# Fourteen expert pieces of a spiking MetaFormer block set into the slots of its last gating groups

## What is computed

```
x = x + conv(ln_c(x))          # q, k, v = lif(xf @ W.T); attention without softmax; lif(y); lif(y @ Wp.T + bp)
t = tokens of x
xt = ln_t(t)
gate = softmax(xt @ Wg);  topv, topi = top_k(gate, 2);  topv = topv / (sum(topv) + 1e-6)
for e in range(8):
    h = gelu(xt @ W1[e] + b1[e])          # 128 -> 512
    ye = h @ W2[e] + b2[e]                # 512 -> 128
    out = out + ye * scores[:, e]
return t + out
```

## Time and profile before

| | |
|---|---|
| median of 3 runs | 544.33 us (542.35 to 544.41) |
| the profiled execution: its time and its span | 544.11 us, 542.4 us |
| TensorE busy, share | 345.3 us, 64% |
| VectorE | 400.4 us, 74% |
| ScalarE | 274.1 us, 51% |
| GpSimd | 221.6 us, 41% |
| mean granted TensorE clock | 0.776 of 2.4 GHz |

### The profile page before, as it was taken

The page is one execution under the profiler, slowest core; times in us unless marked ns, Lnnn a source line. Parts: engine busy times, 40 slices in busy tenths (PEclk is TensorE's granted clock), DMA queues, the critical chain, the costliest instruction groups (busy, mean ns, idle before and its releaser), DMA issues.

```text
span 542.4 us, 10627 instructions
## 1 busy us (share of the span) xinstructions
PE 345.3 (64%) x2516; PEld 285.8 (53%) x2516; DVE 400.4 (74%) x1384; ACT 274.1 (51%) x581; POOL 221.6 (41%) x233
## 2 busy tenths in 40 slices
PE   2456654654644766254420499999999999999200
PEld 2233232432422534133320399999999999999200
DVE  4799999999999599998862356666666666666186
ACT  3436362554525435243230267666677777666073
POOL 3000000007274017374777145566666666666400
PEclk9877677776776576655555599999999999999855
DMA  6901000002121012121354222222222222221299
GB/s 180 274 15 17 16 15 16 16 15 61 41 59 42 9 21 68 42 65 45 98 181 124 74 55 77 71 69 71 71 77 64 76 71 67 70 69 50 68 351 303
DMA packets 62123, 43.05 MB, mean 79 GB/s; under 512 B 29057, under 2 KB 56745, under 8 KB 62096
## 3 DMA queue, kind: packets, MB, share of 16 engines
q1 hardware_dynamic: 53648, 28.85, 20.2%
q0 software_dynamic: 6720, 12.97, 7.6%
q10 hardware_dynamic: 1728, 0.94, 0.6%
HBM read 22.09 MB, written 19.91 MB: 77 GB/s over the span
## 4 chain that ended last, share of the span: by engine, by line
PE 43%; DVE 42%; issue 4%; ACT 3%; POOL 3%; DMA 3%; ACTq 1%; POOLq 0%; SPq 0%; DVEq 0%
PE PS L1172 18%; DVE U L892 7%; DVE VV L884 7%; DVE H_all L872 6%; PE PS L1162 6%; PE PS L1164 5%; PE PS L1163 5%; DVE stats L630 3%; DVE KV L708 3%; POOL by_expert L427 3%; PE PS L1149 2%; PE PS L1105 2%; DVE X L1006 2%; DVE spikes L902 2%; DVE X L1010 1%
## 5 line engine op out<-in xcount | busy, mean ns | idle before, releaser
L427 POOL DMA_INDIRECT by_expert<-XG,place x98 | 97.3, 993 | 197.7 <-DVE place L794 169.3
L443 POOL DMA_INDIRECT by_token<-osp,target x112 | 119.5, 1067 | 89.9 <-DVE osp L976 55.9
L1172 PE MATMUL PS<-w_now,hid 128*128 128x128 f32 x896 | 108.8, 275 | 0.0
L1172 PEld LDWEIGHTS PS<-w_now,hid 128*128 128x128 f32 x896 | 104.8, 192 | 0.0
L560 ACT ACTIVATE hid<-PS,b1c 128x256 f32<-128x256 f32 x224 | 88.2, 480 | 5.1 <-PE PS L1164 2.9
L1162 PE MATMUL PS<-rows_high,w_high 128*128 128x256 f32 x224 | 69.1, 308 | 0.9 <-DVE rows_low L960 0.3
L1164 PE MATMUL PS<-rows_high,w_low 128*128 128x256 f32 x224 | 64.1, 286 | 0.0
L1163 PE MATMUL PS<-rows_low,w_high 128*128 128x256 f32 x224 | 64.0, 286 | 0.0
L566 ACT ACTIVATE w_now<-W_s 128x512 f32 x56 | 35.6, 635 | 54.5 <-PE PS L1172 45.5
L1042 PE MATMUL PS<-xT,wT 128*128 128x392 f32 x96 | 54.4, 693 | 0.7 <-ACT xT L488 0.7
L954 DVE CAST w_high<-H_all 128x512 fp32r x56 | 24.1, 431 | 40.0 <-PE PS L1164 38.7
(11 more groups left out here) (156 smaller groups left out, 570.7 us busy)
## 6 DMA issues: line engine op xcount, KB each, us to landing
rows_in<-by_expert SPq DMA_DIRECT2D x56, 130.0 KB, 2.1
...
```

The source lines that it names most:

```text
L427: pool.indirect_dma_start(by_expert, bass.IndirectOffsetOnAxis(ap=place[g % SENDING][:, k, r:r + 1], axis=0), XG[g % SENDING][:, r, :], No ...
L443: pool.indirect_dma_start(by_token, bass.IndirectOffsetOnAxis(ap=target[b][:, a:a + 1], axis=0), rows_out[b][:, a, :], None, bounds_check= ...
L1172: m = pe.matmul(PS[:, 4 + b % 2, a * 128:a * 128 + 128], hid[b % 2][:, hb, a * 128:a * 128 + 128], w2_now[b % 2][:, hb * C:hb * C + C], st ...
```

## The change

The first 14 pieces hold only rows of groups 0 to 2 (`EARLY` = 14, full pieces of 256 rows), and their loads wait for those groups' scatters alone. The plan is split: `plan_early` in the points of slot 13, `plan_late` in those of slot 21. In slot 16 the pieces 0 and 1 are set up and the `up` of piece 0 is made. Then `EARLY_SLOT` says which pieces stand in which slot: two in each of the slots 17 to 20, four in slot 21. The call for piece j holds the turning of the rows of piece j + 2, `up` of j + 1 and `down` of j. `SEND_SLOT` puts the sends of pieces 0 to 3 behind the scatter of group 7; the others follow the scatter of group 8. The pieces from 12 on follow behind the slots, written out one by one, without loops. In all pieces ScalarE now rounds rows and W1 (`round_rows`, `round_w1`), VectorE makes the remaining parts, and `down` takes W2 from where it lies, at an address from a register that TensorE loads itself; `set_w2` is gone. W1 is loaded in slot 15 into a part of `xT`, and 12 output tiles stand in the place of 4.

```diff
+    EARLY_SLOT = {BLOCKS + 1: (None, 0, None, 1), BLOCKS + 2: (None, 2, None, 3), BLOCKS + 3: (None, 4, None, 5),
+                  BLOCKS + 4: (None, 6, None, 7), BLOCKS + 5: (8, 9, 10, 11)}
+    SEND_SLOT = {BLOCKS + 4: range(0, 4)}
+    PLAN_SLOT, PLAN_FROM = norm2_slot[EARLY_GROUP] + 2, 6
+    SENT_EARLY = max(r.stop for r in SEND_SLOT.values())
+    assert END == BLOCKS + 6 and PLAN_SLOT < BLOCKS
+    def early(slot, k):
+        its = EARLY_SLOT.get(slot, ())
+        return [j for j in its[k:k + 1] if j is not None]
     assert all(norm2_slot[g] < norm2_slot[g + 1] for g in range(GATES - 1))
...
+        target = [sb(f"target{i}", [128, HALVES], I32) for i in range(PIECES)]
...
+            def load_piece(j):
+                start = sp.value_load(piece_start[0:1, j:j + 1], min_val=0, max_val=E * CAP)
+                if j >= DEEP:
+                    sp.wait_ge(piece_read, j - DEEP + 1)
+                sp.dma_start(rows_in[j % DEEP][:], by_expert[bass.ds(start, ROWS), :]
+                             .rearrange("(p a) c -> p a c", a=HALVES)).then_inc(piece_in[j % DEEP], 16)
...
             sp.wait_ge(pieces_ready, 1)
+            for g in range(EARLY_GROUP + 1):
+                sp.wait_ge(scattered[g % SENDING], sent_until(g + SENDING))
+            for j in range(EARLY):
...
+            sp.dma_start(by_expert[E * CAP:E * CAP + ROWS, :].rearrange("(p a) c -> p a c", a=HALVES),
+                         pad_rows[:]).then_inc(padded, 16)
+            sp.wait_ge(pieces_ready, 2)
             sp.wait_ge(padded, 16 * (E + 1))
             for i in range(SENDING):
                 last = max(g for g in range(GATES) if g % SENDING == i)
                 sp.wait_ge(scattered[i], sent_until(last + SENDING))
...
+            def send(j):
+                pool.wait_ge(piece_read, j + 1)
+                pool.wait_ge(rows_ready, j + 1)
+                for a in range(HALVES):
+                    pool.indirect_dma_start(by_token, bass.IndirectOffsetOnAxis(
+                        ap=target[j][:, a:a + 1], axis=0), rows_out[j % OUTS][:, a, :], None,
+                        bounds_check=last_row, oob_is_err=False).then_inc(rows_sent[j % OUTS], 16)
...
             for slot in range(-1, END):
                 for g in gate_group(slot, 2):
                     scatter(g)
-
-
-            last_row = pool.alloc_register("last_row")
-            pool.reg_mov(last_row, 2 * TOK - 1)
...
+            def round_w1(j):
+                act.wait_ge(pieces_ready, 1 if j < EARLY else 2)
+                if j >= 2:
+                    act.wait_ge(up_done, HB * (j - 1))
+                e = expert_on_act(j)
+                nc.scalar.activation(w1_high[j % 2][:], W1_s.rearrange("p e h -> p (e h)")[:, bass.ds(e * HID, HID)],
+                                     ACT.Copy).then_inc(w1_rounded, 1)
+            def gelu(j):
+                e = expert_on_act(j)
+                if j >= 2:
+                    act.wait_ge(down_done, j - 1)
+                for hb in range(HB):
+                    act.wait_ge(up_done, HB * j + hb + 1)
+                    nc.scalar.activation(hid[j % 2][:, hb, :], up_bank(j, hb), ACT.Gelu,
+                                         bias=b1c[:, bass.ds(e * HB + hb, 1)]).then_inc(gelu_done, 1)
...
+            def round_rows(j):
+                act.wait_ge(piece_turned, j + 1)
+                if j >= 2:
+                    act.wait_ge(up_done, HB * (j - 1))
+                nc.scalar.activation(rows_high[j % 2][:], turn_bank(j), ACT.Copy).then_inc(rows_rounded, 1)
+            def piece_on_act(j):
+                if j + AHEAD < PIECES:
+                    round_rows(j + AHEAD)
+                if j + 1 < PIECES:
+                    gelu(j + 1)
+                if j + 3 < PIECES:
+                    round_w1(j + 3)
             for slot in range(-1, END):
                 if slot < 0:
                     spread(0, 0)
...
+                if slot == BLOCKS:
+                    act.wait_ge(w1_in, 16)
+                    for j in range(AHEAD):
+                        round_w1(j)
+                    round_rows(0)
+                    piece_on_act(-1)
+                for j in early(slot, 1):
+                    piece_on_act(j)
+                if slot > BLOCKS:
+                    for x_ in norms(slot):
+                        spread(*x_)
+                for j in early(slot, 2):
+                    piece_on_act(j)
                 if slot >= 0:
                     for x_ in norms(slot):
                         normalise(*x_)
                 for it in ring[slot][1]:
                     copy_item(it)
...
+            def piece_stage(j, stage):
+                n, b = j + AHEAD, (j + AHEAD) % 2
+                if stage == 4:
+                    if j >= 1:
+                        add_b2(j - 1)
+                elif n >= PIECES:
+                    return
+                elif stage == 0:
+                    v.wait_ge(rows_rounded, n + 1)
+                    v.tensor_tensor(rows_low[b][:], turn_bank(n), rows_high[b][:].bitcast(F32),
+                                    ALU.subtract).then_inc(piece_copied, 1)
+                elif stage == 1:
+                    e = expert_on_vector(n)
+                    v.wait_ge(w1_rounded, n + 1)
+                    v.tensor_tensor(w1_low[b][:], W1_s.rearrange("p e h -> p (e h)")[:, bass.ds(e * HID, HID)],
+                                    w1_high[b][:].bitcast(F32), ALU.subtract).then_inc(w1_set, 1)
+                elif stage == 2:
+                    v.scalar_tensor_tensor(target[n][:], rows_in[n % DEEP][:, :, C + 1], piece_rank[:, n:n + 1],
+                                           rows_in[n % DEEP][:, :, C], ALU.not_equal, ALU.add).then_inc(piece_read, 1)
...
+            def point_work(slot, point):
+                norm_stage(slot, point)
+                gate_stage(slot, point)
+                if slot == PLAN_SLOT:
+                    plan_early(point - PLAN_FROM)
+                if slot == BLOCKS and point == 15:
+                    v.wait_ge(pieces_ready, 1)
+                    v.wait_ge(w1_in, 16)
+                if slot == BLOCKS and point >= 16:
+                    piece_stage((point - 16) // 4 - AHEAD, point % 4)
+                for j in early(slot, point // 6):
+                    piece_stage(j, point % 6)
+                if slot == END - 1:
+                    plan_late(point - PLAN_FROM)
...
+            def down(j, a):
+                e = pe.value_load(piece_expert[0:1, j:j + 1], min_val=0, max_val=E - 1)
+                w2 = W2_s[:].rearrange("p e b c -> p (e b c)")
+                if a == 0:
+                    if j >= 2:
+                        pe.wait_ge(rows_ready, j - 1)
+                    pe.wait_ge(gelu_done, HB * (j + 1))
+                for hb in range(HB):
+                    m = pe.matmul(down_bank(j)[:, a * 128:a * 128 + 128], hid[j % 2][:, hb, a * 128:a * 128 + 128],
+                                  w2[:, bass.ds(e * (HB * C) + hb * C, C)], start=(hb == 0), stop=(hb == HB - 1))
+                if a == HALVES - 1:
+                    m.then_inc(down_done, 1)
+            def piece_products(j):
+                if j + AHEAD == EARLY:
+                    pe.wait_ge(ring_copied, len(item_rank))
+                    pe.wait_ge(filled_ready, GATES)
+                    pe.wait_ge(res_added, GATES)
+                if j + AHEAD < PIECES:
+                    turn_piece(j + AHEAD)
+                for half in range(2):
+                    if j + 1 < PIECES:
+                        up(j + 1, half)
+                    if j >= 0:
+                        down(j, half)
...
+                for j in early(slot, 0):
+                    piece_products(j)
                 for g in gate_group(slot, 1):
                     logits(g)
                 for it in ring[slot][0][first:]:
                     ring_item(it)
                 if 1 <= slot <= BLOCKS:
                     query(slot - 1)
+                if slot == BLOCKS:
+                    pe.wait_ge(y_copied, BLOCKS)
+                    pe.wait_ge(pieces_ready, 1)
+                    turn_piece(0)
+                    piece_products(-1)
+                for k in (1, 2):
+                    for j in early(slot, k):
+                        piece_products(j)
                 for it in ring[slot][1]:
                     ring_item(it)
+                for j in early(slot, 3):
+                    piece_products(j)
                 for g in gate_group(slot, 1):
                     count_before(g)
```

425 lines of the change are left out of this document (229 added, 196 removed).

## The result

The changed kernel took 558.5 us (median of four runs, 557.96 to 562.14), the kernel before 543.4 (542.35 to 544.41): a ratio of 1.029, 95% interval 1.024 to 1.034. The profiled execution took 557.96 us for a span of 555.6.

A forecast was written before the change was run, and what follows sets the result against it. GpSimd was taken to bound the kernel up to 305 us, then TensorE to 505.5. Piece 14 turned at 359.4, plus 151.9 late phase, 36.9 sums and stores and 1.7, gave 549.9: forecast 550 us, range 535 to 564.

The forecast's parts named there:

- the likeliest case: The prediction's own account, pieces lengthening the serial chain of each round: 545 to 556 us, chance 0.47.
- piece 0 turned: Slot 16: the first piece's rows, loaded behind the last transpose of `y`, reach TensorE for turning at 256.7 us.
- from there to the end of the count of group 4: Slot 16: turnings, roundings, table load, gelu, `up`, normalised rows and transposes take until 266.2, 9.5 us.
- three rounds: Slots 17 to 19, count to count with two pieces each: 19.7 us a round, 59.1 together; before about 8 each.
- count of group 7 to the last scatter: GpSimd behind the rounds: places 0.9, six scatters 7.6, eight sends 11.1, seven pitches 8.9; last scatter starts at 353.8.
- last scatter to piece 14 turned: From the last scatter's start to TensorE turning piece 14: 5.55 us as before, so at 359.4.
- late phase: Remaining 44 piece calls on TensorE from piece 14's turning: 151.9 us, 48.5 shorter than before.
- sums and stores, and around the span: After TensorE's end: 36.9 us of sums and stores, unchanged, plus 1.7 from span to execution time.
- The early plan: `plan_early`, some 20 small dependent VectorE steps in slot 13: adds 2.8 us, bounds 0 and 6, part hidden in gaps.
- the cold first piece: First call of the late phase, starting at low clock after a wait: 5.9 us, between 3.44 and 6.4.
- The register loads on TensorE's queue: Two per late piece, costed at nothing; rival that they are not hidden: 593 us, half of it 571, chance 0.08.
- the root stands behind the gelus: Slots 17 to 19: ScalarE's root queues behind the piece's gelus; gelu, W1 rounding, table load and root take 2.7 us.

## Why the prediction missed

The sign was right, and so was the mechanism: each round of slots 17 to 19 becomes one chain through three engines, GpSimd gets holes and the sends on top, and the shorter late phase doesn't pay for it. What failed is the size: 15 us were lost where 6 were forecast. The sum was 8.1 us too low against the profiled execution (549.9 and 557.96), and the median lies 2.5 us above the likeliest case's own range. By its steps, in us, with the second traced execution of the changed kernel (558.26 us) beside the first:

| step | forecast | measured | difference | second |
|---|---|---|---|---|
| piece 0 turned | 256.7 | 258.4 | +1.7 | 261.2 |
| from there to the end of the count of group 4 | 9.5 | 11.8 | +2.3 | 11.8 |
| three rounds | 59.1 | 58.3 | -0.8 | 57.1 |
| count of group 7 to the last scatter | 28.5 | 29.1 | +0.6 | 29.4 |
| last scatter to piece 14 turned | 5.55 | 9.05 | +3.5 | 8.2 |
| late phase | 151.9 | 152.2 | +0.3 | 151.8 |
| sums and stores, and around the span | 38.6 | 39.2 | +0.6 | 38.8 |

**The term that failed most** is the 5.55 us "as before" behind the last scatter. It took the scatters to be what the load of piece 14 waits for. The diff had given four pads to ScalarE behind `round_w1(14)`, which waits for the whole late plan; I counted neither. It is 9.05 us, and 8.2 in the second execution. The pads are 2.9 and 2.0 of that, by the kernel with the pads on SyncE, which has 6.2.

**The early plan** was put at 2.8 between bounds of 0 and 6. It is 5.6 (5.3 in the second execution), near the upper bound: its steps hid in hardly any gap of VectorE. The first line of the table shows less than the term was off, since this execution reached the count of group 2 1.3 us earlier than the kernel before (193.57 and 194.82). The second one reached it at 195.74, and there the first line is +4.5, the largest of all.

**The setup of slot 16** took 2.3 more than its sum: the steps come as written down (turning, table load, second half of `up`, normalised rows), with waits of 1.0, 1.3 and 1.8 us on TensorE where another engine hands over to it (the second turning, the second half of `up`, the transposes). TensorE's 8.75 us wait for `rows_in` ahead of it is the one forecast.

**Right**: the rounds together (19.7 each, 19.4 in the mean, at mean granted clocks of 0.63, 0.90 and 0.74, between the levels as assumed; that the mean fits so well is in part luck, since the single ones take 21.7, 17.2 and 19.4), the late phase, the cold first piece (5.9, 5.74 measured), 3.43 us a piece and no stall at the loop's turn. The register loads on TensorE's queue are hidden; on VectorE such a load still takes 309 ns (308 before). The Trainium skill ("DMA: Bandwidth & Descriptors", latency and other measured facts) gives a floor of about 600 ns; the trace has half of that.

**Right, but not the whole cause**: "the root stands behind the gelus". It does, in slots 17 and 19 by 4.5 and 3.5 us behind its variance. But ScalarE's order is only one of three: in slot 18 VectorE's variance is hardly earlier, and TensorE's queue has the piece's products ahead of the transposes in each slot. With the root alone moved the rounds took 3.5 us longer.
